# Three-part stacks of the first attention gathered by transfers from one transpose of q and k

## The reference

```python
def attn(xin):
    qkv = (xin @ Wqkv.T + qkv_bias).reshape(Bs, Lx, 3, H, D)
    ...
    sm = jnp.exp(jnp.minimum(scale_mul_log, jnp.log(jnp.float32(100.0))))
    qn = q / jnp.maximum(jnp.linalg.norm(q, axis=-1, keepdims=True), 1e-12) * sm
    kn = k / jnp.maximum(jnp.linalg.norm(k, axis=-1, keepdims=True), 1e-12)
    scores = jnp.einsum('bhqd,bhkd->bhqk', qn, kn) + attn_bias
    p = jax.nn.softmax(scores, axis=-1)
    o = jnp.einsum('bhqk,bhkd->bhqd', p, v)
    ...
    return o @ Wproj.T + bproj
x = x + attn(_ln(x) * (scale1 + 1.0) + shift1) * gamma1
h = _gelu_tanh((_ln(x) * (scale2 + 1.0) + shift2) @ Wfc1.T + bfc1)
x = x + (h @ Wfc2.T + bfc2) * gamma2
```

## Time and profile before

| | |
|---|---|
| median of 3 runs | 290.06 us (289.78 to 291.6) |
| the profiled execution | 290.29 us |
| its span, first to last instruction | 287.8 us |
| mean granted TensorE clock | 0.972 of full |
| busy: PE / PE weight loads / DVE / ACT / POOL | 253.5 / 206.5 / 208.3 / 164.5 / 118.2 us |

### The profile page before, as it was taken

One profiled execution on the slowest core, in us unless ns is written; L12 is line 12 of the kernel. 1 busy time (PEld: TensorE's weight loads), 2 busy tenths in 40 slices (PEclk: granted clock), 3 DMA queues, 4 the chain that ended last, 5 costly groups with the idle time before them and its releaser, 6 DMA issues.

```text
span 287.8 us, 5303 instructions
## 1 busy us (share of the span) xinstructions
PE 253.5 (88%) x1934; PEld 206.5 (72%) x1934; DVE 208.3 (72%) x453; ACT 164.5 (57%) x291; POOL 118.2 (41%) x185
## 2 busy tenths in 40 slices
PE   0669897879998999999599999999899999999973
PEld 0547575537766678687499999998788778887852
DVE  4167778999985959968678869678986997926322
ACT  2110476457698999669777478804529364482440
POOL 3814856945134005169762045652553726100000
PEclk9999579999999999999999999999999999999996
DMA  5970000005300000003010000000000000100012
GB/s 156 388 215 0 3 1 0 0 1 180 118 2 6 2 3 4 0 7 110 5 36 3 0 2 0 2 0 0 3 1 3 0 0 2 39 0 2 0 36 74
DMA packets 8250, 10.13 MB, mean 35 GB/s; under 512 B 1824, under 2 KB 7072, under 8 KB 8224
## 3 DMA queue, kind: packets, MB, share of 16 engines
q1 hardware_dynamic: 8224, 9.79, 10.5%
HBM read 8.61 MB, written 1.05 MB: 34 GB/s over the span
## 4 chain that ended last, share of the span: by engine, by line
PE 61%; ACT 13%; DVE 11%; issue 8%; DMA 3%; POOL 2%; SPq 1%; ACTq 0%; DVEq 0%; POOLq 0%
PE ring L795 10%; PE ring L797 9%; PE ring L796 9%; PE ring L801 9%; PE psx L873 4%; PE ring L848 4%; DVE nm L1195 3%; PE pv L893 3%; ACT kstk L681 3%; ACT kstk L680 3%; DMA stage_a<-in_wada 2%; PE ring L1046 2%; PE psx L1070 2%; PE pv L1096 2%; ACT kstk L759 2%
## 5 line engine op out<-in xcount | busy, mean ns | idle before, releaser
L606 ACT ACTIVATE ps<-psx 128x1024 f32<-128x1024 f32 x40 | 39.4, 1027 | 16.9 <-PE psx L1075 8.5
L1195 DVE TENSOR_REDUCE nm<-ring 128x2 f32<-128x512 f32 x64 | 39.8, 683 | 2.1 <-PE ring L848 2.1
L801 PE MATMUL ring<-ident,stack 128*128 128x128 f32 x224 | 30.2, 277 | 3.6 <-ACT kstk L681 1.5
L801 PEld LDWEIGHTS ring<-ident,stack 128*128 128x128 f32 x224 | 24.3, 141 | 8.8 <-issue 4.3
L795 PE MATMUL ring<-wqkv_hi,xm_hi 128*128 128x512 f32 (+1 forms) x64 | 24.6, 385 | 4.7 <-DVE wqkv_lo L1147 4.3
L848 PE MATMUL ring<-kstk,qstk 128*128 128x512 f32 x64 | 24.2, 440 | 3.7 <-ACT kstk L681 1.6
L447 POOL TENSOR_TENSOR rstd<-ve,half_neg 128x2 f32<-128x2 f32 x12 | 9.7, 817 | 38.5 <-DVE ve L1164 25.3
L796 PE MATMUL ring<-wqkv_lo,xm_hi 128*128 128x512 f32 (+1 forms) x64 | 23.3, 363 | 0.0
L797 PE MATMUL ring<-wqkv_hi,xm_lo 128*128 128x512 f32 (+1 forms) x64 | 23.1, 361 | 0.0
L596 ACT ACTIVATE xmt<-ring,mod 128x256 f32<-128x256 f32 x16 | 8.1, 559 | 25.8 <-PE ring L801 25.8
L873 PE MATMUL psx<-qstk,kstk 128*128 128x256 f32 x128 | 20.4, 291 | 0.5 <-DMA qstk<-stage_a 0.2
(11 more groups left out here) (199 smaller groups left out, 758.2 us busy)
## 6 DMA issues: line engine op xcount, KB each, us to landing
xs<-in_x SPq DMA_DIRECT2D x4, 256.0 KB, 8.3
stage_a<-in_wada SPq DMA_DIRECT2D x4, 256.0 KB, 7.3
stage_a<-in_wfc SPq DMA_DIRECT2D x1, 1024.0 KB, 5.3
stage_b<-in_wfc SPq DMA_DIRECT2D x1, 1024.0 KB, 7.4
out<-x SPq DMA_DIRECT2D x4, 256.0 KB, 2.2
row<-in_rows SPq DMA_DIRECT2D x1, 906.0 KB, 9.3
stage_b<-in_wqkv SPq DMA_DIRECT2D x1, 768.0 KB, 7.6
stage_a<-in_wqkv SPq DMA_DIRECT2D x1, 768.0 KB, 4.5
```

The source lines that it names most:

```text
L606: a.activation(ps[:, n % 4], psx[:, n % 2], ACT.Exp).then_inc(exp_done, 1)
L801: last = nc.tensor.transpose(dst[:, i * P:(i + 1) * P], src, ident[:, :])
L1195: v.tensor_reduce(nm[:, qc, :, p], bank(key).rearrange("p (h n) -> p h n", h=2), AX.X, ALU.max, negate=True).then_inc(ring_dve, 1)
```

## The change

The rows of q and k are transposed once, as 4 blocks of 128 columns a tile (`turn0`, 4 transposes into one ring bank, key `T0`). ScalarE copies the bank to `turned` as its high part (one copy of 128x512), VectorE writes the low part (bank minus high, one of 128x512). The stacks are then put together by transfers of SyncE: `stack0` issues 12 transfers of 128 KB a batch, each from 64 partitions of `turned` into 16 partitions of `qstk` or `kstk`: 8 for the high parts once both tiles' high copies are there, 4 for the low parts once both banks are emptied. For a transfer to find what it wants, the columns of Wqkv, of its bias and of the scales are sorted on the host (`by_slot`); on the core, `sums0` and `unit0` then view `qn` with another stride.

The zeros and ones in the slots, which `const_stack` wrote, come from `blank` (part of x2, filled by `const_rows`): four transfers of 128 KB and four of 16 KB once, and two of 16 KB more for each of batches 2 and 3. `max0` waits for the transfers of its batch instead of ScalarE's copies. `ORDER` is another list throughout, and SyncE walks it too. `const_sel` moves behind `mask` on GpSimd, `gamma` behind the maxima of batch 0.

```diff
-        stack = sb("stack", [P, TB, 2 * H0, SLOT], F32R)
+        split_buf = sb("split_buf", [P, 2, HC * L], F32R)
...
+            def blank_rows(buf, s, which, n, done):
+                for par in range(2):
+                    sp.dma_start(stack_row(buf, par, 48, n, s), blank[0:PAIRS * n, which, :]).then_inc(done, 16)
+
+            def stack_parts(s, w, places, done):
+                for buf, c, j in places:
+                    for par in range(2):
+                        sp.dma_start(stack_row(buf, par, D0 * j, D0, s),
+                                     turned[SLOT * par:SLOT * par + SLOT, s, w, c:c + 2, :].bitcast(F32))\
+                          .then_inc(done, 16)
...
+                if name == "const_rows":
+                    sp.wait_ge(blank_ready, 1)
+                    for s in range(2):
+                        blank_rows(qstk, s, 0, SLOT - 48, s_rows[s])
+                    for s in range(2):
+                        sp.wait_ge(kzero_ready, s + 1)
+                        blank_rows(kstk, s, 1, 2, s_rows[s])
+                if name == "stack0":
+                    if b >= 2:
+                        sp.wait_ge(s_full, PAIRS * (b - 1))
+                        blank_rows(qstk, b % 2, 0, 2, s_rows[b])
+                    sp.wait_ge(turned_hi, TB * (b + 1))
+                    stack_parts(b % 2, 0, ((qstk, 0, 0), (qstk, 0, 1), (kstk, 2, 0), (kstk, 2, 2)), s_stack[b])
+                    sp.wait_ge(*emptied(("T0", TB * b + 1)))
+                    stack_parts(b % 2, 1, ((qstk, 0, 2), (kstk, 2, 1)), s_stack[b])
...
-                if name == "hi0":
-                    act.wait_ge(qn_ready, t + 1)
...
-                if name == "turnk0":
...
+                if name == "turn0":
+                    act.wait_ge(*full(("T0", t)))
+                    if b >= 2:
+                        act.wait_ge(s_stack[b - 2], 16 * 12)
+                    a.activation(turned[:, b % 2, 0, :, i_ * P:i_ * P + P], bank(("T0", t)).rearrange("p (c n) -> p c n", c=4),
+                                 ACT.Copy).then_inc(turned_hi, 1)
...
                 if (qc, p) == (0, 0):
-                    for w in ("qT", "kT"):
-                        pe.wait_ge(*emptied((w, TB * b + 1, 1)))
+                    pe.wait_ge(s_rows[b], 16 * (4 if b < 2 else 2))
+                    pe.wait_ge(s_stack[b], 16 * 12)
...
-                        step(v.tensor_reduce(ss[:, t % TB, :], qn[:, t % TB, :].rearrange("p (h d) -> p h d", d=D0),
-                                             AX.X, ALU.add))
+                        step(v.tensor_reduce(ss[:, t % TB, :].rearrange("p (g q) -> p g q", q=4),
+                                             qn[:, t % TB, :].rearrange("p (g d q) -> p g q d", d=D0, q=4), AX.X, ALU.add))
...
+                if name == "turn0":
+                    dve.wait_ge(turned_hi, t + 1)
+                    dve.wait_ge(*full(("T0", t)))
+                    v.tensor_tensor(turned[:, b % 2, 1, :, tok], bank(("T0", t)).rearrange("p (c n) -> p c n", c=4),
+                                    turned[:, b % 2, 0, :, tok].bitcast(F32), ALU.subtract)\
+                     .then_inc(ring_dve, 1)
```

## The result

The changed kernel takes 310.2 us in the median (309.1 to 311.7), the kernel before 289.9: 1.070 times as long, 95% interval 1.064 to 1.075. The forecast of 285 us was wrong, and the time lies 7 us above the range too. What happened is the mechanism of the second rival, and it cost more time than the 301.5 us of that rival's sum. (All ratios in this text leave out executions disturbed by a lower granted clock, and medians count them: two of four in `spread`, and three of seven in `merge_again`, whose median is 289.4 us against 289.7 before.)

A forecast was written before the change was run, and what follows sets the result against it. No engine alone bounds the attention; removed transposes pay until VectorE binds. Lead 3.8 us at first scores, 6.0 by batch 3's maxima, less 1.5 waits, 4.5, rounded to 5: 290.1 - 5 = 285 us; range 280 to 303.

The forecast's parts named there:

- the second rival: Stack transfers: a narrow target of 16 partitions makes them the bound, 1.1 us each; 301.5 us, chance 0.32.
- I take 0.64 us, the issue of the nearest transfer: Price of one 128 KB stack transfer, taken from the shift rows' issue; range 0.4 to 1.2 us.
- a quarter of what all sixteen would be allowed: Argument against the narrow target: the shift rows' two partitions take 27 GB/s, a quarter of sixteen's allowance.
- The break-even at 0.75 us: Price per stack transfer near which the change would neither gain nor lose; at 0.8 us the sum gave 291.
- step 2: First scores to batch 3's maxima: 35 to 36 us, lead 6.0 us, less 1.5 of stack waits: 4.5.
- Step 1: Up to the first scores: first maxima at about 51 us, first scores at 67.5 against 68.8, lead 3.8 us.
- Removed work: Per-instruction savings: TensorE 12.5 us of transposes, ScalarE 35 us of copies, VectorE 2 us in all.
- The stride at nothing: Wider stride in `sums0` and `unit0` costed at zero; rival: doubled reductions cost 3 us more, 288, chance 0.08.
- What would show it: Listed trace signs: right, DMA waits of 1 to 3 us in all; wrong, `kstk` waits over 5 us three times.

The follow-up runs named there:

- spread: Changed kernel with stack rows dealt out, each transfer's 16 target partitions four apart instead of neighbouring: 293.1 us, ratio 1.016 to the kernel before.
- merge_again: The kernel of merge measured once more, unchanged: 289.4 us, ratio 0.990 to the kernel before.
- early: Changed kernel with the blank rows sent before batch 0's stack: 304.1 us, ratio 1.052 to the kernel before.
- merge: Changed kernel with dealt-out rows, early blank rows and both halves' q transfers joined into one of 256 KB: 288.0 us, ratio 0.993 to the kernel before.
- flat2: As merge, but reductions of the squares read neighbouring elements (wrong columns, same work): 287.6 us, ratio 0.995 to the kernel before.
- hold2: Changed kernel with 36, 22 and 24 filler products on TensorE before its waits for the stacks of batches 0, 2, 3: 308.8 us, ratio 1.064.
- merge_gam: As merge, with the four gamma products moved in front of the first maxima: 299.4 us, ratio 1.029 to the kernel before.
- merge_warm: As merge, with one filler product on TensorE ahead of each of batch 0's maxima but the first: 290.1 us, ratio 0.999 to the kernel before.

## Why the prediction was wrong, step by step

Starts in us, from the timelines of the profiled executions:

| | before | after | early | spread | merge |
|---|---|---|---|---|---|
| first maxima | 48.2 | 57.4 | 50.6 | 49.8 | 48.6 |
| first scores | 68.8 | 75.3 | 68.2 | 67.4 | 66.4 |
| maxima of batch 2 | 91.6 | 106.5 | 99.0 | 93.3 | 91.6 |
| maxima of batch 3 | 111.6 | 127.5 | 120.6 | 108.5 | 105.6 |
| last score matmul | 137.5 | 157.2 | 150.9 | 137.4 | 134.5 |
| span | 287.8 | 307.3 | 300.7 | 287.4 | 284.2 |

- **The step that failed is "I take 0.64 us, the issue of the nearest transfer".** An issue is no price for moving the bytes. The issue costs 0.63 us, and moving 128 KB into 16 neighbouring partitions costs 1.02 us (129 GB/s at a share of 1.13). I had the row, 27 GB/s into two partitions, and its two readings. The first, that sixteen partitions then take eight times as much, would be 216 GB/s and is excluded; the second, a neighbourhood of four, gave 1.2 us and was off by 0.18. The argument that decided me ("a quarter of what all sixteen would be allowed") treated the two partitions' speed as spread evenly, which no row said. The Trainium skill, "SBUF — State Buffer", section "Door 1: The DMA port swizzle", states 104 GB/s for a load of 1 MiB into partitions 0 to 15. The chip showed 129 to 132 with transfers alternating between the two halves, a quarter more, and the rule is right in kind: it spoke against the change, and I gave that rival 0.32.
- **The break-even at 0.75 us was too high.** At 1.02 us the change loses, as it said. But with the issue as the limit, 0.64 us, the sum gave 285 us, and `spread` takes 1.016 times the time before; only its quickest execution reaches the span before (287.4 against 287.8). So a second step fails too, step 2 below.
- **Step 1.** TensorE was ready for the first maxima at 48.9 us, not 51, and the transfers landed at 57.4; the rival had 58.6 for them. With the target wide, the first scores start at 67.4 us in `spread` and at 66.4 in `merge`, where the forecast had 67.5: this step holds.
- **Step 2.** The waits in front of batches 2 and 3, forecast at 1.5 us together (10.5 by the rival), were 5.2 and 6.1. `merge` has neither, and yet the other term of the step, "35 to 36 us" from the first scores to batch 3's maxima, is 3 us short: they are 39.1 us apart there (66.4 to 105.6). VectorE is busy for 32.5 of them, 83%, where I had 31, 86% or more (and the earlier trace rows has VectorE at 91% from 48.2 to 68.8 us, so "not over 90%" was no reading of the rows). At batch 3's maxima `merge` is 111.6 - 105.6 = 6.0 us ahead, but the kernel before has issued 72 score matmuls there and `merge` 64. Eight are two steps, the 2.1 us that my sum subtracts. (Counted from the timelines of L873 and L884.) So the lead is 3.9 us where the sum had 6.0, and it stays near that: 3.0 at the last score matmul, 3.6 at the end. Why the stretch takes 39 us no run took apart. It isn't the stride (`flat2`: 38.0 us there and the same time), and the clock in it is 0.98:

```profile
66.40:105.60 39.20, 35.43 (x284) 24.44 (x283) 32.54 (x64) 21.13 (x26) 8.54 (x20) 0.98 0.33 111
```

- **The rival's sum of 301.5 us was 8.7 too low,** though its price of 1.1 us was above the 1.02 measured. Some 4.5 us are the base: without waits the sum stands at 283.5 us, and `merge`, which has none, takes 288.0. The rest is waits. Against `merge`, the changed kernel is 8.8 us late at the first maxima (7.5 in the rival's sum), 14.9 at batch 2's (6.1 more; 6.5), 21.9 at batch 3's (7.0 more; 4) and 23.1 at the end. So 3 us are stack 3, which I had waiting less because the batch before it was late already. But as `early` shows, each stack's release moves with the scores, so no wait covers another. Whether the half clock adds to this is open: the 1.5 us of `hold2` aren't clear of noise.
- **Removed work.** ScalarE's busy time fell from 164.5 to 133.2 us, 31 of the 35 forecast, and bought little: of the 16 us of `kstk` copies on the chain, only 3.6 came out at the end of `merge`. The turned copies take 0.60 and 0.69 us as costed. VectorE's busy time did not fall by 2 us but rose by 5.8 (208.3 to 214.1): 2.2 were removed as forecast, 3.1 came with the stride, and 4.9 net with operations whose shape is unchanged. The largest of them is L1174, on eight tiles (before as L1178: mean 439 ns):

```profile
L1174 DVE TENSOR_SCALAR xh<-xs,mv,rstd 128x256 f32<-128x256 f32 x8 | 7.5, 972 | 0.1
```

  All of it is in the first two of the eight, which take 1.44 and 3.84 us; the other six take 0.39 to 0.48. They stand at 6.3 and 7.7 us, where the changed list has GpSimd fill `vs` and `kstk`:

```profile
6.33 5.20 DVE L1174 TENSOR_SCALAR xh<-xs,mv,rstd 128x256 f32<-128x256 f32 x2
...
7.83 3.55 POOL L514 MEMSET kstk<- 128x4096 f32 x1
```

  No run moved the fill, so the cause isn't shown. It stands ahead of the attention.
- **The stride at nothing: right,** with another size than either side had. 1.08 us a reduction against 0.68, not twice. The Trainium skill, same page, "Door 1", its remark on cachelines, is borne out in kind, since the reductions at that stride are slower by 0.40 us each. The time doesn't show it (0.993 for `merge`, 0.995 for `flat2` without the stride): other work covers it.
- **What would show it.** The list held: waits for `kstk` over 5 us three times (8.6, 5.2, 6.1), DMA at 9 tenths in the blocks (three of them, not four, at 129 to 132 GB/s). Single issues did stretch: of the 48 of the stacks two took 1.62 us (at 40.4 and 97.6 us) and one 1.01, the others about 0.6. But a wide target has such issues too (1.15 and 1.22 us in `spread`), so they don't tell a narrow one.

## To carry to other kernels

An on-chip transfer has two prices, the issue on its queue and the bytes at its target, and only the second depends on where the bytes go: before replacing copies by transfers, count how many groups of neighbouring partitions each one writes, and if the order of rows is free (as in a contraction), deal them out; a spacing of four was enough here, and no other was tried. Check the bound with the one narrow transfer that the trace does have, and take the pessimistic reading when nothing but evenness speaks for the other. When a step is moved ahead of others, look up every producer it waits for in the new list: `merge_gam` took 11 us more than `merge`, behind a matrix that had always been ready before.

## What the runs showed of the hardware

- The same 128 packets of 1 KB, sent to 16 partitions four apart, ran at 193 GB/s with the DMA engines 0.60 busy, against 129 to 132 at 1.1 busy for 16 neighbours. So the "busy" share of a DMA engine also holds its waiting for the target.
- A transfer of 256 KB into 32 partitions four apart costs the issuing engine as much as one of 128 KB into 16, 0.6 us, and lands after 2.5 us instead of 2.3 (`merge`).
- In `hold2` TensorE's clock was at its upper level through 8 us of filling, and fell to half at the end of the sixteen maxima that followed, one per 0.6 us.
- Filling TensorE's idle time kept the clock up there and moved the fall elsewhere: in `hold2` and `merge_warm` 32 value products behind the attention took 3.62 and 3.33 us instead of 1.93.
